# Routed feed-forward weights as four 32-column tiles with the shared matrix added on GpSimd, routing steps moved to the start, the bias split in attention, inputs ahead of constants

## The chip, the cores and the metric

One core of one Trainium2 chip runs the kernel as one program. The metric is the device time of one execution in microseconds (us), lower is better. The engines are named PE (TensorE, with its weight loads as PEld), DVE (the vector engine), ACT (ScalarE), POOL (GpSimd) and SP (SyncE, which issues the DMAs).

## The reference, cut to what matters

The input is 64 sequences of 375 frames with 16 features. Each is cut into 45 overlapping patches and projected to 64 features; then come four residual blocks, each behind a layer norm: attention (8 heads of 8), a dense top-2 mixture of 8 experts, a delta-rule recurrence, and the routed feed-forward block that the change is about:

```python
h = jax.nn.relu(flat @ Wi.T + bi)
for l in range(n_layers):                      # 2 layers
    shared = (jnp.einsum('nd,shd->snh', h, Ws[l]) + bs[l][:, None, :]).mean(axis=0)
    routed = jnp.zeros_like(h)
    for e in range(n_experts):                 # 16 experts, one per sequence
        ye = h @ Wr[l, e].T + br[l, e]
        routed = routed + jnp.where((route == e)[:, None], ye, 0.0)
    h = jax.nn.relu(shared + routed + h)
out = h @ Wo.T + bo
```

The expert is chosen per sequence by `route_id`, so all 45 tokens of a sequence use one 128x128 matrix `Wr[l, e]`; `Ws[l]` is shared by all; the residual `h` is an identity matrix more.

## The kernel before, in words

All activations stay in SBUF in one tensor `arena`, features on partitions, two sequences side by side (partitions 0 to 63 and 64 to 127). The 64 sequences are 32 such pairs in 4 chunks (`C`) of 8 pairs (`PP`); a chunk has `W` = 360 columns (8 pairs x 45 tokens `T`). `a(c, off, n)` is a piece of chunk `c`, `slot(i)` its i-th piece of 360 columns; `bank(c, b)` is one of its two PSUM banks. `K` holds the constants, in five groups that five DMAs load; `k(name)` is one of them.

The order of the work is one list, `ORDER` (lines 82 to 138), of steps (name, index, chunk). Every engine walks the same list and issues its own part of each step, so each engine's queue is in that order, and semaphores tie them together. Most stages run chunk 0, 1, 2, 3 of one step, then of the next. Attention (lines 99 to 112) runs 32 units (pair i, chunk c): step `t` transposes the probabilities, `s` makes the next scores (PE), their maximum and difference (DVE, lines 591 and 593), `e` the exponential (ACT, line 377), and `pv`, two units later, the weighted values. The recurrence (`m`, `lx`, `lt`, `u`, `y2`, `z`, `w`, `o`) works on 45x45 blocks per sequence. Each fp32 matrix product appears in the profile as two passes, each a weight load and a matmul. All products but the transposes (line 827) have line 763.

What the change touches:

- SP (lines 230 to 263): constants group 0, input chunk 0, group 1, the mask constants, input chunks 1 to 3, the route ids twice (`rid` on one row, `ridb` on 51), then groups 2, 3, 4. When DVE has made the expert indices `ride` (semaphore `r_id`), SP loads one 128x128 matrix for each of the 64 sequences and both layers (line 258): layer 0 into `WG0`, layer 1 into the arena behind `WG1_`, the latter once that chunk's attention is done (`h1`).
- POOL: after clearing buffers (lines 272 to 274) it adds the identity to both shared matrices (line 280); then come sums of the rotary products (285, 288), the 32 key products of attention (291) and later steps.
- DVE: `route_ids()` (lines 508 to 535) is called after the last value step of attention (line 587). Seven instructions (512 to 523) make `ride` and the one-hot matrix `oneh`; four more (527 to 534) split the biases into three bf16 parts, `rb_split`.
- PE, step `r` (lines 1005 to 1021), once per layer `i` and chunk `c`. For each of two banks j: one bf16 product adds the bias over all 360 columns, eight fp32 products of a sequence's 128x128 matrix with its 45 columns follow, and one fp32 product of the shared matrix (identity added) with all 360 columns ends the sum. ACT rectifies both banks (line 495).
- PE waits in step `f` for `r_oh`, `rb_split` and `wsI`, and in `r` for the weight DMAs.

## Time and profile before

| what | value |
|---|---|
| median of 3 runs | 418.08 us |
| lowest | 417.31 us |
| profiled execution, first to last instruction | 417.9 us |
| PE busy | 359.1 us (86%), 4976 passes |
| DVE busy | 226.4 us (54%) |
| ACT busy | 198.2 us (47%) |
| POOL busy | 112.6 us (27%) |
| DMA | 14.82 MB, mean 35 GB/s |

One of the three runs took 674.59 us, so only the median and the lowest are used. What the profiled execution took beyond its span is not listed; the median is 0.2 us above the span. Busy time of an engine says how long it had instructions in flight; the share is of the span. A timeline row gives start, length, engine, line, operation, tensors (out<-in), partitions x elements and a count, and in brackets the idle time before it and who ended it. The shape of a PE row reads rows*columns of the weights, then rows x columns of the moving operand.

### The profile page before, as it was taken

How to read it: one execution, taken by the hardware profiler on the slowest of the kernel's cores; microseconds unless marked ns; L12 is line 12 of the kernel's file. 1: busy time of each engine (PE TensorE's matmuls, PEld its weight loads, DVE VectorE, ACT ScalarE, POOL GpSimd, SP SyncE). 2: the span in 40 equal slices, each digit the busy share in tenths (PEclk: the TensorE clock that was granted, in tenths of full speed). 3: DMA queues.
4: the chain of work that ended last, by engine and by line, in shares of the span. 5: the costliest groups of instructions: out<-in, count | busy, mean ns of one | idle time of the engine just before them, and what ended most of it. 6: DMA issues, size and time to landing. Idle time of an engine off the chain costs nothing.

```text
span 417.9 us, 11928 instructions
## 1 busy us (share of the span) xinstructions
PE 359.1 (86%) x4976; PEld 247.0 (59%) x4976; DVE 226.4 (54%) x446; ACT 198.2 (47%) x382; POOL 112.6 (27%) x138
## 2 busy tenths in 40 slices
PE   4999839999997799999587947878776997999997
PEld 1447726677775534343244527878776993477774
DVE  3277797787646743333693999946663038500002
ACT  1574235444447356776747792570008645531110
POOL 9009991000000036465133026880000003000000
PEclk9999969999998699999959995999999898899999
DMA  7400012222212122121000000000000000000001
GB/s 280 192 0 2 5 38 57 60 59 59 65 54 61 55 62 59 58 64 57 20 0 0 2 0 2 3 4 5 5 5 3 3 5 0 2 0 2 0 2 71
DMA packets 20558, 14.82 MB, mean 35 GB/s; under 512 B 2329, under 2 KB 19353, under 8 KB 20377
## 3 DMA queue, kind: packets, MB, share of 16 engines
q1 hardware_dynamic: 20504, 14.07, 10.7%
q8 instruction: 39, 0.64, 0.7%
q14 instruction: 15, 0.11, 0.1%
HBM read 13.32 MB, written 0.74 MB: 34 GB/s over the span
## 4 chain that ended last, share of the span: by engine, by line
PE 54%; DVE 18%; POOL 11%; issue 8%; ACT 7%; DMA 1%; SPq 0%; POOLq 0%; DVEq 0%
PE PS L763 49%; POOL arena L298 7%; PE PS L827 4%; DVE arena L710 3%; DVE arena L566 2%; DVE arena L549 2%; POOL arena L321 2%; DMA arena<-xT 1%; ACT arena L356 1%; ACT arena L353 1%; POOL arena L317 1%; ACT arena L468 1%; POOL arena L316 1%; DVE arena L713 1%; ACT arena L472 1%
## 5 line engine op out<-in xcount | busy, mean ns | idle before, releaser
L763 PE MATMUL PS<-arena,K 128*128 128x360 f32 (+2 forms) x608 | 163.1, 513 | 21.5 <-DVE arena L566 6.4
L763 PE MATMUL PS<-arena 128*45 128x45 f32 (+6 forms) x3264 | 129.9, 227 | 21.3 <-ACT arena L448 9.7
L763 PEld LDWEIGHTS PS<-arena 128*45 128x45 f32 (+3 forms) x3264 | 111.7, 133 | 40.1 <-issue 23.9
L763 PEld LDWEIGHTS PS<-arena,K 128*128 128x128 f32 (+2 forms) x608 | 75.8, 183 | 82.5 <-issue 22.1
L298 POOL TENSOR_TENSOR arena<-arena 128x360 f32<-128x360 f32 x32 | 30.0, 948 | 105.9 <-DVE arena L672 105.2
L672 DVE TENSOR_TENSOR arena<-PS,arena 128x360 f32<-128x360 f32 x32 | 17.1, 533 | 33.7 <-ACT arena L402 33.7
L763 PE MATMUL PS<-K,arena 128*45 128x32 f32 (+4 forms) x768 | 26.1, 223 | 5.1 <-DVE arena L655 4.4
L763 PEld LDWEIGHTS PS<-K,arena 128*45 128x45 f32 (+2 forms) x768 | 25.3, 132 | 7.0 <-DVE arena L655 5.0
L827 PE MATMUL PS<-K,arena 128*128 128x128 f32 x128 | 21.5, 292 | 7.8 <-ACT arena L377 7.7
L756 DVE SCALAR_TENSOR_TENSOR arena<-PS,K,arena 128x360 f32<-128x360 f32 x4 | 2.4, 593 | 47.2 <-PE PS L763 47.2
L380 ACT COPY arena<-PS 128x360 f32<-128x360 f32 x32 | 14.9, 468 | 25.5 <-PE PS L827 25.4
L398 ACT ACTIVATE arena<-PS,K 128x720 f32<-128x720 f32 x32 | 24.9, 862 | 2.5 <-PE PS L763 2.5
L291 POOL TENSOR_TENSOR arena<-arena,K 128x360 f32<-128x360 f32 x32 | 24.6, 813 | 0.0
L495 ACT ACTIVATE arena<-PS 128x720 f32<-128x720 f32 x8 | 6.2, 771 | 38.6 <-PE PS L763 38.6
L324 POOL TENSOR_TENSOR arena<-arena 128x360 f32<-128x360 f32 x4 | 4.4, 1110 | 70.6 <-DVE arena L557 70.6
L543 DVE TENSOR_TENSOR arena<-arena,PS 128x360 f32<-128x360 f32 x24 | 12.3, 528 | 19.3 <-PE PS L763 18.3
L402 ACT COPY arena<-PS 128x360 f32<-128x360 f32 x32 | 14.8, 463 | 14.8 <-PE PS L763 14.8
L591 DVE TENSOR_REDUCE smax<-PS 128x8 f32<-128x360 f32 x32 | 17.0, 531 | 8.7 <-PE PS L763 8.6
L377 ACT ACTIVATE arena<-arena 128x360 f32<-128x360 f32 x32 | 16.4, 512 | 10.9 <-DVE arena L593 10.9
L549 DVE TENSOR_TENSOR arena<-arena 128x360 f32<-128x360 f32 x24 | 12.7, 531 | 14.8 <-ACT arena L356 14.8
L468 ACT ACTIVATE arena<-arena,K 128x360 f32<-128x360 f32 x8 | 4.3, 589 | 34.4 <-DVE arena L745 34.4
L827 PEld LDWEIGHTS PS<-K,arena 128*128 128x128 f32 x128 | 14.2, 145 | 10.2 <-ACT arena L377 8.2
(124 smaller groups left out, 422.8 us busy)
## 6 DMA issues: line engine op xcount, KB each, us to landing
WG<-wr SPq DMA_DIRECT2D x64, 64.0 KB, 1.9
arena<-wr SPq DMA_DIRECT2D x64, 64.0 KB, 1.9
arena<-xT SPq DMA_DIRECT2D x4, 368.0 KB, 6.4
K<-consts SPq DMA_DIRECT2D x1, 1171.0 KB, 12.3
K<-consts SPq DMA_DIRECT2D x1, 852.0 KB, 9.9
out<-arena SPq DMA_DIRECT2D x4, 180.0 KB, 1.9
K<-consts SPq DMA_DIRECT2D x1, 510.0 KB, 5.5
K<-consts SPq DMA_DIRECT2D x1, 352.0 KB, 12.4
```

The costliest lines, as they stand in the source:

```text
L291: g.tensor_tensor(a(c, KX_ + i * W).rearrange("q (h t) -> q h t", t=T), a(c, slot(4) + i * T, T).unsqueeze(1).broadcast_to([128, NH, T]), ...
L298: g.tensor_tensor(a(c, H_), a(c, H_), a(c, slot(3 + i % 2)), ALU.add).then_inc(sem["acc"], 1)
L377: s.activation(pb, pb, ACT.Exp).then_inc(sem["s_exp"], 1)
L380: s.copy(a(c, PT_, 512).rearrange("q (r t) -> q r t", t=64)[:, :, 0:T], bank(c, 1, 512).rearrange("q (r t) -> q r t", t=64)[:, :, 0:T]).th ...
L398: s.activation(halves(a(c, slot(6), 2 * W)), both(c), ACT.Gelu, bias=k("b1", i, i + 1)).then_inc(sem["gelu"], 1)
L402: s.copy(a(c, slot(8)), bank(c, 1)).then_inc(sem["cwb"], 1)
L549: v.tensor_tensor(a(c, dst), a(c, xc), a(c, sq), ALU.mult).then_inc(sem["ln_out"], 1)
L591: v.tensor_reduce(smax[:, c, :], sc, AX.X, ALU.max).then_inc(sem["s_max"], 1)
L672: v.tensor_tensor(a(c, slot(3 + i % 2)), bank(c, 0), a(c, slot(8)), ALU.mult).then_inc(sem["y_mul"], 1)
L710: v.scalar_tensor_tensor(out=kr[:, :, 0, 1:T], in0=pair(a(c, slot(3)))[:, :, 1:T], scalar=vec(f"feat{j}"), in1=pair(a(c, slot(13)))[:, :, ...
L763: return nc.tensor.matmul(o, l, r, start=start, stop=stop)
L827: last = nc.tensor.transpose(bank(c, 1, 128, 128 * g), a(c, PB_ + 128 * g, 128), k("identf"))
```

## The change

1. The eight fp32 products of a bank are each cut into four, with 32 columns of the weights and 32 output partitions each. Their sum no longer gets the product with the shared matrix, and both bias products come ahead of all of them.
2. POOL adds the shared matrix (with the identity) to all 16 loaded matrices of a chunk and layer in one instruction of 128x2048 elements, eight in all: those of layer 0 after the last key product of attention, those of layer 1 at the recurrence's first `lx` step. PE's `r` waits for that (`wsum`) in place of the DMAs.
3. The identity sums on POOL move from the start to behind the last key product.
4. `route_ids()` comes first on DVE, before the first layer norm, and loses the four split instructions; these (`split_biases()`) come after the 17th unit's values in attention.
5. SP issues all four input chunks and the route ids ahead of constants group 1 and the masks, and group 4 ahead of 2 and 3.

```diff
             load_consts(0)
             for c in range(C):
                 sp.dma_start(a(c, XT_, 2 * PP * CH), xT[:, c, :]).then_inc(sem[f"x{c}"], 16)
-                if c == 0:
-                    load_consts(1)
-                    sp.dma_start(KB[:], masks_bf).then_inc(sem["cst_bf"], 16)
...
+            load_consts(1)
+            sp.dma_start(KB[:], masks_bf).then_inc(sem["cst_bf"], 16)
+            for g in (4, 2, 3):
...
+            def shared_plus_identity():
...
+                for l in range(NL):
+                    ws = k("Ws", 128 * l, 128 * l + 128)
+                    g.tensor_tensor(ws, ws, k("identf"), ALU.add).then_inc(sem["wsI"], 1)
+            def add_shared(l, c):
+
+                pool.wait_ge(sem["wsI"], l + 1)
+                pool.wait_ge(sem[f"wg{l}_{c}"], 16 * 2 * PP)
+                w = WG0[:, 2 * PP * c:2 * PP * (c + 1), :] if l == 0 else a(c, WG1_, 2 * PP * 128).rearrange(
+                    "q (b n) -> q b n", n=128)
+                shared = k("Ws", 128 * l, 128 * l + 128).unsqueeze(1).broadcast_to([128, 2 * PP, 128])
+                g.tensor_tensor(w, w, shared, ALU.add).then_inc(sem["wsum"], 1)
...
+                    if (i, c) == (PP - 1, C - 1):
+                        shared_plus_identity()
+                        for cc in range(C):
+                            add_shared(0, cc)
...
+                elif name == "lx" and i == 0:
+                    add_shared(1, c)
...
+            route_ids()
...
-                    if c == C - 1:
-                        route_ids()
...
+                    if (i, c) == (PP // 2, 0):
+                        split_biases()
...
-                        pe.wait_ge(sem["wsI"], NL)
...
-                    pe.wait_ge(sem[f"wg{i}_{c}"], 16 * 2 * PP)
+                    pe.wait_ge(sem["wsum"], n)
                     src = slot(2 if i == 0 else 4)
                     for j in range(2):
                         mm(pair(bank(c, j)), rb_split[:, 1, 128 * i:128 * i + 128],
...
+                    for j in range(2):
                         for p in range(PP):
                             b = PP * j + p
-                            w = WG0[:, 2 * PP * c + b, :] if i == 0 else a(c, WG1_ + 128 * b, 128)
-                            mm(bank(c, j, T, p * T), w, a(c, src + j * W + p * T, T), start=False, stop=False)
-                        last = mm(bank(c, j), k("Ws", 128 * i, 128 * i + 128), a(c, src + j * W), start=False)
+                            for lo in range(0, 128, 32):
+                                w = WG0[:, 2 * PP * c + b, lo:lo + 32] if i == 0 else a(c, WG1_ + 128 * b + lo, 32)
+                                last = mm(bank(c, j, T, p * T, lo, lo + 32), w, a(c, src + j * W + p * T, T), start=False,
+                                          stop=(p == PP - 1))
```

How the instructions stand, first on PE for the routed step of one chunk in layer 0, before (`oneh` is the one-hot matrix, `WG0` the loaded matrices; a row counts products, each of which is one or two passes):

```order
L763 MATMUL PS<-arena,K 128x360 x28
L763 MATMUL PS<-oneh,rb_split 128x360
L763 MATMUL PS<-arena,WG0 128x45 x8
L763 MATMUL PS<-arena,K 128x360
L763 MATMUL PS<-oneh,rb_split 128x360
L763 MATMUL PS<-arena,WG0 128x45 x8
L763 MATMUL PS<-arena,K 128x360
```

and now, two chunks:

```order
L785 MATMUL PS<-arena,K 128x360 x28
L785 MATMUL PS<-oneh,rb_split 128x360 x2
L785 MATMUL PS<-arena,WG0 32x45 x64
L785 MATMUL PS<-oneh,rb_split 128x360 x2
L785 MATMUL PS<-arena,WG0 32x45 x64
```

The 16 products with 128 output rows and the two shared ones of a chunk have become 64 products with 32 output rows.

On DVE, the end of the value steps and the start of attention's units, before (`ride` is what SP waits for):

```order
L516 TENSOR_SCALAR oneh<-ridb,K 51x64
L519 TENSOR_TENSOR arena<-arena 1x64
L521 TENSOR_TENSOR arena<-arena 1x64
L523 TENSOR_SCALAR ride<-arena 1x64
L527 CAST rb_split<-K 51x256
L529 SCALAR_TENSOR_TENSOR K<-rb_split,K 51x256
L532 CAST rb_split<-K 51x256
L534 SCALAR_TENSOR_TENSOR rb_split<-rb_split,K 51x256
L591 TENSOR_REDUCE smax<-PS 128x8
```

and now the first instructions of DVE, with the split in the middle of attention:

```order
L523 TENSOR_SCALAR oneka<-K 128x1
L529 TENSOR_SCALAR arena<-rid 1x64
...
L540 TENSOR_SCALAR ride<-arena 1x64
L565 TENSOR_TENSOR arena<-arena,PS 128x360 x4
...
L623 TENSOR_TENSOR arena<-PS,orec 128x64
L548 CAST rb_split<-K 51x256
L550 SCALAR_TENSOR_TENSOR K<-rb_split,K 51x256
L553 CAST rb_split<-K 51x256
L555 SCALAR_TENSOR_TENSOR rb_split<-rb_split,K 51x256
L611 TENSOR_REDUCE smax<-PS 128x8
```

All eleven stood ahead of attention's first maximum; none does now.

On POOL, the rotary sums, the key products and what follows them, before:

```order
L280 TENSOR_TENSOR K<-K 128x128 x2
L285 TENSOR_TENSOR arena<-arena 128x360 x4
L288 TENSOR_TENSOR arena<-arena 128x360 x4
L291 TENSOR_TENSOR arena<-arena,K 128x360 x32
L298 TENSOR_TENSOR arena<-arena 128x360 x32
```

and now:

```order
L296 TENSOR_TENSOR arena<-arena 128x360 x4
L299 TENSOR_TENSOR arena<-arena 128x360 x4
L302 TENSOR_TENSOR arena<-arena,K 128x360 x32
L281 TENSOR_TENSOR K<-K 128x128 x2
L290 TENSOR_TENSOR WG0<-WG0,K 128x2048 x4
L313 TENSOR_TENSOR arena<-arena 128x360 x32
```

The four sums into the loaded matrices stand between the key products and the mixture's accumulations.

## Rows read from the trace of the kernel before

**Rows 1.** The page's first line.

```profile
span 417.9 us, 11928 instructions
```

**Rows 2.** Who TensorE waited for: us in total, times, longest us.

```profile
PE PS L763 <- issue: 6.6, 10, 0.8
...
PE PS L763 <- DVE PS L503: 5.3, 1, 5.3
```

**Rows 3.** Timeline, routed stage, layer 0, chunk 0: start us, us, instructions.

```profile
366.71 0.32 PE L763 MATMUL PS<-oneh,rb_split 51*128 51x360 bf16 x1
...
366.96 1.98 PE L763 MATMUL PS<-arena,WG 128*128 128x45 f32 x16
...
368.76 0.85 PE L763 MATMUL PS<-arena,K 128*128 128x360 f32 x2
...
369.55 0.33 PE L763 MATMUL PS<-oneh,rb_split 51*128 51x360 bf16 x1
```

**Rows 4.** The same view, ScalarE: the last rectification of the routed stage.

```profile
412.37 0.77 ACT L495 ACTIVATE arena<-PS 128x720 f32<-128x720 f32 x1 [4.92 <-PE PS L763]
```

**Rows 5.** Timeline, vector engine and TensorE, before attention's first transposes.

```profile
48.82 0.79 DVE L512 TENSOR_SCALAR arena<-rid 1x64 f32<-1x64 int32 x1
...
54.06 0.28 DVE L527 CAST rb_split<-K 51x256 bf16<-51x256 f32 x1
...
56.10 0.89 DVE L534 SCALAR_TENSOR_TENSOR rb_split<-rb_split,K 51x256 bf16<-51x256 bf16 x1
...
56.91 0.52 DVE L591 TENSOR_REDUCE smax<-PS 128x8 f32<-128x360 f32 x1
...
58.60 1.11 PE L827 MATMUL PS<-K,arena 128*128 128x128 f32 x4 [7.67 <-ACT arena L377]
```

**Rows 6.** The same view: the last of the first four score products.

```profile
50.16 0.77 PE L763 MATMUL PS<-arena 128*128 128x360 f32 x2
```

**Rows 7.** Engines' busy time by stretch; PEclk is the granted clock.

```profile
60.00:61.00 1.00, 1.00 (x3) 0.37 (x2) 0.97 (x3) 0.51 (x1) 1.00 (x2) 0.50 0.21 63
...
61.00:62.00 1.00, 1.00 (x7) 0.98 (x6) 0.73 (x3) 0.92 (x3) 1.00 (x2) 0.78 0.21 61
```

**Rows 8.** Timeline, attention in its steady part, two successive maxima.

```profile
72.81 0.53 DVE L591 TENSOR_REDUCE smax<-PS 128x8 f32<-128x360 f32 x1 [0.32 <-PE PS L763]
...
74.61 0.53 DVE L591 TENSOR_REDUCE smax<-PS 128x8 f32<-128x360 f32 x1 [0.32 <-PE PS L763]
```

**Rows 9.** Timeline of the first 16 us: products of the four input chunks.

```profile
5.25 2.68 PE L763 MATMUL PS<-arena,K 128*64 128x360 f32 x8 [5.25 <-DVE PS L503]
...
8.90 11.28 PE L763 MATMUL PS<-arena,K 128*64 128x360 f32 x40 [0.97 <-DMA arena<-xT]
...
13.95 0.56 ACT L344 ACTIVATE arena<-PS,K 128x360 f32<-128x360 f32 x1 [1.75 <-PE PS L763]
...
15.18 0.56 ACT L344 ACTIVATE arena<-PS,K 128x360 f32<-128x360 f32 x1 [0.67 <-PE PS L763]
```

**Rows 10.** Timeline of TensorE, recurrence: two unbroken runs of 128 passes.

```profile
289.97 2.92 PE L763 MATMUL PS<-arena 128*45 128x45 f32 x128 [0.81 <-issue]
...
293.43 2.92 PE L763 MATMUL PS<-arena 128*45 128x45 f32 x128 [0.54 <-issue]
```

**Rows 11.** DMA queues from 286 to 319 us: packets, MB, share.

```profile
q8 instruction: 9, 0.15, 2.0%
```

**Rows 12.** Timeline of TensorE, recurrence output, 64-column weights.

```profile
336.80 7.06 PE L763 MATMUL PS<-arena 128*64 128x45 f32 x235
```

**Rows 13.** Timeline of TensorE, the values of attention.

```profile
37.72 10.06 PE L763 MATMUL PS<-K,arena 128*45 128x32 f32 x256
```

**Rows 14.** Line 258: count, duration ns min/median/max, first and last start.

```profile
L258 SPq DMA_DIRECT2D WG<-wr x64: 332/333/1192, 55.1 to 127.6; - x64
```

**Rows 15.** GpSimd: key products in the timeline; then groups by line.

```profile
39.78 24.62 POOL L291 TENSOR_TENSOR arena<-arena,K 128x360 f32<-128x360 f32 x32
...
L324 POOL TENSOR_TENSOR arena<-arena 128x360 f32<-128x360 f32 x4 | 4.4, 1110 | 70.6 <-DVE arena L557 70.6
```

More of the change, by code:

```diff
@@ L64 @@
 SEMS = """rb_steps r_steps g_steps cst0 cst1 cst2 cst3 cst4 cst_bf ids psum0 init oneka rb_split
-r_id r_oh wsI
+r_id r_oh wsI wsum
 tok_mm tok_y h0 ln_mean ln_xc ln_sq ln_var ln_log ln_rs ln_out
@@ L238, in _ @@
                 sp.dma_start(a(c, XT_, 2 * PP * CH), xT[:, c, :]).then_inc(sem[f"x{c}"], 16)
-                if c == 0:
-                    load_consts(1)
-                    sp.dma_start(KB[:], masks_bf).then_inc(sem["cst_bf"], 16)
             sp.dma_start(rid[:], route[0:1, :]).then_inc(sem["ids"], 16)
             sp.dma_start(ridb[:], route[0:1, :].broadcast_to([3 * (NR + 1), B])).then_inc(sem["ids"], 16)
-            for g in (2, 3, 4):
+            load_consts(1)
+            sp.dma_start(KB[:], masks_bf).then_inc(sem["cst_bf"], 16)
+            for g in (4, 2, 3):
                 load_consts(g)
@@ L274, in _ @@
                 g.memset(a(c, VD_, PP * 2 * NKV * 18), 0.0).then_inc(sem["init"], 1)
-            pool.wait_ge(sem["cst4"], 16)
-            pool.wait_ge(sem["cst1"], 16)
-            for l in range(NL):
-                ws = k("Ws", 128 * l, 128 * l + 128)
-                g.tensor_tensor(ws, ws, k("identf"), ALU.add).then_inc(sem["wsI"], 1)
+            def shared_plus_identity():
+                pool.wait_ge(sem["cst4"], 16)
+                pool.wait_ge(sem["cst1"], 16)
+                for l in range(NL):
[8 more added lines that the diff above has]
+                g.tensor_tensor(w, w, shared, ALU.add).then_inc(sem["wsum"], 1)
             for name, i, c in ORDER:
@@ L523, in route_ids, with split_biases @@
                 v.tensor_scalar(ride[:], rtmp[:, 0, :], float(NR), None, ALU.add).then_inc(sem["r_id"], 1)
+            def split_biases():
+                rows = 3 * (NR + 1)
                 dve.wait_ge(sem["cst4"], 16)
```

## The prediction

> **What bounds the kernel now.** I began with the length of the span, 417.9 us [rows 1], then asked who TensorE waits for. It is in flight 86% of the time, and the named waits are small; the interesting ones are 6.6 us on "issue", in ten pieces, and 5.3 us at the start for the clearing of PSUM [rows 2]. So TensorE's own stream is the bound in most stages, and I read three places of the timeline.
>
> First the routed stage. It starts with a bias product at 366.71 [rows 3] and its last rectification starts at 412.37 [rows 4]: 45.7 us for eight steps (4 chunks, 2 layers), 5.7 us each, with nothing between them. Inside one bank, the sixteen passes over 128-column weights take 368.76 - 366.96 = 1.80 us, so 112 ns each, although each moves only 45 columns. The shared matrix and the turn to the next bias take 369.55 - 368.76 = 0.79 us, a bias 0.25 us [rows 3]. The stage pays for loading weights, not for streaming.
>
> Second the start of attention. From 48.82 to 56.91 the vector engine makes route ids and splits biases; only then comes the first maximum, and TensorE starts the first transposes at 58.60 after 7.67 us of idleness [rows 5]. The scores that the maximum reads were long there: the last of the first four ended at 50.16 + 0.77 = 50.93 [rows 6]. After the pause the granted clock is 0.50 (the 1.2 GHz level) and returns within the stretch 61 to 62, whose mean is 0.78 [rows 7].
>
> Third the first 16 us: TensorE begins at 5.25, when PSUM is clear, and then waits 0.97 us for input chunk 1 [rows 9].
>
> **The routed stage, part by part.** Removed per step: 32 passes over 128 columns and 4 over the shared matrix. Added: 128 passes with 32-column weights and the same 45 moving columns. Nothing in this trace has 32-column weights cycling over four column tiles. The nearest rows are the recurrence's: 45-column weights, 45 moving columns, outputs alternating between the two halves of the partitions. There 128 passes take 2.92 us, 22.8 ns each [rows 10]. With 64-column weights, also alternating, 7.06 us for 235 is 30.0 ns [rows 12]. Without alternation, the values of attention, 45-column weights and 32 moving columns: 10.06 us for 256, 39.3 ns [rows 13]. Alternating tiles thus nearly halves the price, so loads into one tile do proceed beside work in the other. I take 22.8 ns, since 32 columns are nearest to 45 and the tiles alternate still more; the bounds are 22.8 below (a cheaper pass stands nowhere in these rows) and 39.3 above.
>
> A step is then 128 x 22.8 ns = 2.92 us, two biases at 0.25 us, and one turn from the small passes back to a bias, at most about 0.5 us (the 0.79 us less 0.3 us for streaming two passes of 360 columns at 2.4 GHz): 3.4 to 3.9 us.
>
> There is a second limit. In rows 10 each run is exactly 128 passes, that is 256 instructions, and is followed by 0.54 to 0.81 us in which TensorE waits for nothing that the profile shows. In the 33 us from 286 to 319 the instruction queue moved 9 packets of 0.15 MB together [rows 11], some 16 KB each; one per 33 / 9 = 3.67 us. I read this as instruction fetch: 128 passes cannot go by in less than about 3.67 us. A step has 130 passes, 3.73 us, as much as its work. I take 3.8 us: 8 x 3.8 = 30.4 us instead of 45.7, a gain of 15.3 us. Bounds: 8 x 3.4 = 27.2 (gain 18.5) and, at 39.3 ns with 1.0 us beside, 8 x 6.03 = 48.2 (a loss of 2.5).
>
> The Trainium skill, page "TensorE: Matmul & The Clock Gate", section on LDWEIGHTS, gives a load as its columns divided by 1.2 per ns. By it 32 columns cost 26.7 ns and four of them as much as one load of 128, so that cutting into tiles saves no load at all; the stage would be an estimated 8 x (3.42 + 1.0) = 35.4 us and the whole 5.0 us later than mine. Rows 12 speak against taking it as a floor for alternating tiles: 64 columns are 53.3 ns by the rule and took 30.0.
>
> **The shared sums on POOL.** A sum over 2048 columns is not in the trace. Key products took 24.62 / 32 = 0.77 us for 360 columns, the dearest sum 1110 ns [rows 15]: per column 2.1 to 3.1 ns, so 4.4 to 6.3 us each, eight of them 35 to 50 us. They are off the path if their inputs come early and POOL has room. Layer 0: POOL is free after its key products, at 39.78 + 24.62 = 64.4; SP needs (127.6 - 55.1) / 63 = 1.15 us per matrix [rows 14], 18.4 us a chunk, and starting near 15 us is done with the fourth chunk near 89. The POOL sums end by about 95, long before POOL's next work in the mixture. Layer 1 sits behind POOL's last work for the recurrence's setup and needs 18 to 25 us from about 280, while `r` wants it from 367 on. Cost on the path: nothing. If POOL were twice as slow there would still be room.
>
> **Route ids and bias split.** With them gone, the first maximum can start at 48.82, its chain to the transposes is 58.60 - 56.91 = 1.69 us long, which gives 50.51; TensorE is busy until 50.93. So the transposes begin there, 7.7 us earlier. And there is no pause, so the half clock from 58.6 to about 61.4 (0.78 is 0.44 us at half and the rest at full) goes too: 2.8 us of work at half speed is 1.4 us. What is late next is TensorE itself.
>
> The seven id instructions move behind the arrival of the ids. They took 54.06 - 48.82 = 5.24 us while POOL was running [rows 5]. The ids now stand behind 1.6 MB instead of 2.4 MB, so I put them near 9 to 10 us; done by 12 to 15. The vector engine is first wanted by the layer norm after the fourth input chunk, near 13 to 14. I count 0, at worst 1.5 us. The four split instructions take 56.91 - 54.06 = 2.85 us in attention. A unit there is 74.61 - 72.81 = 1.80 us, with 0.32 us of idleness of the vector engine [rows 8], and its differences are wanted by transposes four units later. A delay of 2.9 us fits into that distance of 7 us and is caught up at 0.32 us a unit: 0, at worst 2.9.
>
> **Inputs first.** The 0.97 us wait goes. Chunk 3 took 15.18 - 13.95 = 1.23 us, while chunk 0 took 2.68 [rows 9]; the faster passes may also start earlier when TensorE has no break. Between 0.5 and 2.7 us, I take 1.5. Constants group 1 is now behind the inputs but first wanted near 28.
>
> **Sum.** 15.3 + 7.7 + 1.4 + 1.5 = 25.9 us. From the span of 417.9 us that is 392.0; the median stands 0.2 above the span, which I leave within the rounding: 392.
>
> **Rivals.**
> (a) Fetch does not bind and the turns are free, 3.4 us a step: 418 - 10.6 - 18.5 = 389. For it: the first buffer is full when the stage starts. Against: nine fetches in a row at one spacing.
> (b) Four tiles overlap no better than rows 12, 30.0 ns: 8 x (3.84 + 1.0) = 38.7, gain 7.0, time 400. At the 39.3 ns of rows 13: 410, within the noise of nothing gained but attention's part.
> (c) The other side: POOL holds the vector engine for the length of an instruction. For it: tiny instructions on one row took 0.79 us while POOL's key products took 0.77 [rows 5, 15]. Were all vector work held, four sums of 4.4 us or more in attention and four in the recurrence would cost 2 x 17.6 = 35 us there: 427 or more. It decides from the point where over 26 us are held. Against: the maximum took 0.52 us beside a running POOL and 0.53 beside an idle one [rows 5, 8]; what reads PSUM is not held, and in both places nearly all vector work reads PSUM.
> (d) A pass costs what an instruction costs, whatever its columns. At the 112 ns of rows 3 the stage is 8 x (14.3 + 1.0) = 122 us and the time about 418 - 10.6 + 77 = 484; the break-even is (45.7 + 10.6) / 8 - 1.0 over 128, 47 ns. Against: 22.8 ns was reached. The Trainium skill, page "TensorE: Matmul & The Clock Gate", section "Back-to-back issue gap", names some 62 ns per matmul where the sequencer decodes each in software; by that the time would be an estimated 433 us. The trace disagrees by its 22.8 ns.
> (e) The change does not do what it says at the start: ids arrive so late that the first layer norm waits some 4 us: 396.
>
> **How the numbers follow.** Forecast 0.54, (a) 0.17, (b) 0.19 at 400 and 0.03 at 410, (c) 0.03, (d) 0.02, (e) 0.02. A measurement of this kernel can tell about 2% from no change, which is 8.4 us, so faster means below 409.7: 0.54 + 0.17 + 0.19 + 0.02 + 0.01 = 0.93; same 0.04; slower 0.03. The range goes from 386 (case (a) with the full 2.7 us of the start) to 401 (case (b)).
>
> **What would show it.** Right: a routed step of about 3.8 us with gaps of half a microsecond after every 128 passes; TensorE without a pause before the transposes and a granted clock of 1.00 there; SP's weight loads from about 15 us; POOL sums of 4 to 6 us ending before 100 and 310. Wrong: a routed pass above 30 ns, vector instructions in attention longer than 0.55 us while POOL sums run, a wait of `r` for a sum, or a first layer norm later than 15.5 us.

## The result and the profile after

The changed kernel takes 392.52 us, the median of four runs (390.86 to 395.19), against 418.95 us for the kernel before. The ratio is 0.936, 95% interval 0.932 to 0.941: 6.4% faster. The forecast was 392.0 us. The number was right to 0.5 us, but one term of it was not: the price of a pass in the routed stage was put at twice what it is, and instruction fetch, which the prediction also had, held the stage's total. Medians here count every execution, the ratios leave out one slow one each of the kernel before (674.59 us), of two tiles (526.71) and of the old transfers (401.88).

First the page of the changed kernel: its length, the busy times and the granted clock in 40 slices. TensorE is busy 326.8 us instead of 359.1, although it runs 736 more passes; GpSimd is busy 142.3 us instead of 112.6.

```profile
span 393.2 us, 13416 instructions
...
PE 326.8 (83%) x5712; PEld 222.4 (57%) x5712; DVE 220.6 (56%) x446; ACT 197.7 (50%) x382; POOL 142.3 (36%) x146
...
PEclk9999999999997799999959998699999999879996
```

The last digit of the clock row is 6, and was 9 before: the grant is lower at the very end. That is followed up below.

The routed stage in the timeline, the third step of layer 0 and the start of the next. Rows 3 answer to these; lines 785 and 512 are lines 763 and 495 of the kernel before.

```profile
361.89 0.37 PE L785 MATMUL PS<-arena,WG 128*32 128x45 f32 x15 [1.50 <-issue]
...
362.19 0.48 PE L785 MATMUL PS<-oneh,rb_split 51*128 51x360 bf16 x2
...
362.60 1.35 PE L785 MATMUL PS<-arena,WG 128*32 128x45 f32 x111
...
365.99 0.39 PE L785 MATMUL PS<-arena,WG 128*32 128x45 f32 x17 [2.04 <-issue]
...
366.32 0.48 PE L785 MATMUL PS<-oneh,rb_split 51*128 51x360 bf16 x2
```

111 passes run in 1.35 us, then TensorE does nothing for 2.04 us in which it "waits for nothing that the profile shows", then come 17 more, and the step is over. So passes cost 11 to 12 ns, and about half of this step (2.04 of 4.13 us) is a pause in the middle of it. In the successive steps 113, 111, 108, 106, 103, 101 and 98 passes stand ahead of the pause: since a step has 130 passes, the pause comes after every 128, and wanders through the steps. The seven pauses are 1.44 to 2.04 us long, 1.7 us in the mean, and between 357 and 386 us the queue that brings instructions moved seven packets:

```profile
q8 instruction: 7, 0.11, 1.4%
```

The first step has no pause:

```profile
357.15 1.51 PE L785 MATMUL PS<-arena,WG 128*32 128x45 f32 x128
...
358.60 0.48 PE L785 MATMUL PS<-oneh,rb_split 51*128 51x360 bf16 x2
```

It takes 358.60 - 356.75 = 1.85 us. The whole stage, from its first bias at 356.75 to its last rectification, is 385.98 - 356.75 = 29.2 us against 45.7 before.

```profile
385.87 4.39 PE L785 MATMUL PS<-arena,K 128*64 128x360 f32 x16
...
385.98 0.77 ACT L512 ACTIVATE arena<-PS 128x720 f32<-128x720 f32 x1 [3.64 <-PE PS L785]
```

Behind it the last sixteen passes of the kernel take 4.39 us; before they were over in less than 3.4. The tail from the last rectification to the end is 393.2 - 386.0 = 7.2 us; before it was 417.9 - 412.4 = 5.5 [rows 4]. The busy times by stretch say why: the granted clock is 1.00 for most of the stage and 0.62 in its last 4.5 us, where it falls to the 1.2 GHz level, and it is 0.50 until 388 us.

```profile
362.20:381.50 19.30, 10.55 (x657) 8.08 (x652) 0.00 (x0) 3.85 (x5) 0.00 (x0) 1.00 0.01 4
...
381.50:386.00 4.50, 2.85 (x133) 2.27 (x134) 0.00 (x0) 0.79 (x2) 0.00 (x0) 0.62 0.01 4
```

Where this fall comes varies. The changed routed step ran in three more profiles (values alternate, and the old transfers twice). There the clock, over stretches of 2 us, was at 0.50 to 0.59 from 364 to 368, from 368 to 374 and from 378 to 382 us, in the middle of the stage; the stage took 28.6, 29.2 and 27.3 us, and the tail 5.5 us each time. So the 1.7 us of the tail belong to this one execution. In all four TensorE had been idle for much of the time at a grant of 1.00 before the fall (here 8.75 of the 19.3 us from 362.2). The kernels here whose routed stage has no pauses show no such fall in it, save one, the sum alone at full width.

The start of attention, to be held against rows 5 and 6: the first maximum follows the value steps at once, and the transposes (line 849, before 827) begin as soon as TensorE is through the first four scores.

```profile
46.64 0.51 DVE L611 TENSOR_REDUCE smax<-PS 128x8 f32<-128x360 f32 x1
...
47.98 0.77 PE L785 MATMUL PS<-arena 128*128 128x360 f32 x2
...
48.59 0.60 PE L849 MATMUL PS<-K,arena 128*128 128x128 f32 x4
...
52.73 0.65 PE L849 MATMUL PS<-K,arena 128*128 128x128 f32 x4
```

58.60 has become 48.59, 10.0 us earlier. The fourth group of transposes, which stood at 64.16 in the kernel before, starts at 52.73, 11.4 us earlier: the 1.4 us of half clock are gone as well. Of the 10.0 us, 2.2 were there already at the first layer norm, which starts at 13.81 instead of 15.98; 7.8 are the pause.

```profile
5.25 12.76 PE L785 MATMUL PS<-arena,K 128*64 128x360 f32 x48 [5.25 <-DVE PS L520]
...
10.83 0.18 DVE L529 TENSOR_SCALAR arena<-rid 1x64 f32<-1x64 int32 x1 [5.57 <-DMA ridb<-route]
...
11.85 0.18 DVE L540 TENSOR_SCALAR ride<-arena 1x64 int32<-1x64 f32 x1
...
13.01 0.56 ACT L361 ACTIVATE arena<-PS,K 128x360 f32<-128x360 f32 x1 [0.68 <-PE PS L785]
...
13.81 2.34 DVE L565 TENSOR_TENSOR arena<-arena,PS 128x360 f32<-128x360 f32 x4 [1.78 <-PE PS L785]
```

TensorE no longer waits for input chunk 1 [rows 9]. The ids land at 10.8 us, and the seven id instructions take 12.0 - 10.8 = 1.2 us where they took 5.24 [rows 5]; they are done at 12.03, before the vector engine is wanted at 13.81.

The bias split in attention and the one wait it caused, in the timeline of the vector engine and of TensorE:

```profile
82.55 0.28 DVE L548 CAST rb_split<-K 51x256 bf16<-51x256 f32 x1
...
83.69 0.47 DVE L555 SCALAR_TENSOR_TENSOR rb_split<-rb_split,K 51x256 bf16<-51x256 bf16 x1
...
84.09 0.52 DVE L611 TENSOR_REDUCE smax<-PS 128x8 f32<-128x360 f32 x1
...
85.70 0.63 PE L849 MATMUL PS<-K,arena 128*128 128x128 f32 x4 [0.53 <-DVE arena L623]
```

1.5 us of split instead of 2.85, and TensorE waits 0.53 us once for the values' normalisation (line 623).

The sums on GpSimd, in the groups by line:

```profile
L290 POOL TENSOR_TENSOR WG<-WG,K 128x2048 f32<-128x2048 f32 x4 | 15.2, 3816 | 13.2 <-DMA WG<-wr 13.2
...
L290 POOL TENSOR_TENSOR arena<-arena,K 128x2048 f32<-128x2048 f32 x4 | 15.2, 3842 | 0.0
```

3.8 us each, under the 4.4 to 6.3 estimated. The last of layer 0 ends at 90.7, the last of layer 1 at 284.9, 72 us before the routed stage begins. The one real wait among them, 13.2 us, is GpSimd's own for the fourth chunk's matrices, and costs nobody anything.

### The profile page after: what moved, and what is told of

It is laid out like the page before. It is cut to its first block, busy times and chain, and to the rows that moved or that the text cites. A ratio compares the mean times of both kernels' runs of the same rounds, so it can differ in the third digit from the quotient of the medians.

```text
span 393.2 us, 13416 instructions
## 1 busy us (share of the span) xinstructions
PE 326.8 (83%) x5712; PEld 222.4 (57%) x5712; DVE 220.6 (56%) x446; ACT 197.7 (50%) x382; POOL 142.3 (36%) x146
## 4 chain that ended last, share of the span: by engine, by line
PE 52%; DVE 17%; issue 12%; ACT 10%; POOL 8%; POOLq 0%; DVEq 0%
PE PS L785 48%; POOL arena L313 7%; PE PS L849 4%; DVE arena L588 2%; DVE arena L732 2%; DVE arena L571 2%; ACT arena L373 2%; ACT arena L370 1%; ACT arena L476 1%; ACT arena L485 1%; DVE PS L520 1%; ACT arena L489 1%; ACT arena L365 1%; DVE arena L735 1%; DVE arena L584 1%
## 5 line engine op out<-in xcount | busy, mean ns | idle before, releaser
L785 PE MATMUL PS<-arena,K 128*128 128x360 f32 (+2 forms) x576 | 149.7, 515 | 21.2 <-DVE arena L588 7.3
L785 PE MATMUL PS<-arena 128*45 128x45 f32 (+6 forms) x3648 | 118.5, 221 | 31.7 <-issue 15.4
L785 PEld LDWEIGHTS PS<-arena 128*45 128x45 f32 (+4 forms) x3648 | 100.7, 127 | 50.6 <-issue 36.4
L785 PEld LDWEIGHTS PS<-arena,K 128*128 128x128 f32 (+2 forms) x576 | 71.0, 183 | 81.8 <-issue 22.6
L365 ACT ACTIVATE arena<-arena 128x360 f32<-128x360 f32 x24 | 11.8, 503 | 17.1 <-DVE arena L565 15.7
L290 POOL TENSOR_TENSOR WG<-WG,K 128x2048 f32<-128x2048 f32 x4 | 15.2, 3816 | 13.2 <-DMA WG<-wr 13.2
L394 ACT ACTIVATE arena<-arena 128x360 f32<-128x360 f32 x32 | 16.4, 513 | 3.3 <-DVE arena L613 3.3
## 6 DMA issues: line engine op xcount, KB each, us to landing
K<-consts SPq DMA_DIRECT2D x1, 1171.0 KB, 10.7
```

The costliest lines, as they stand in the source:

```text
L290: g.tensor_tensor(w, w, shared, ALU.add).then_inc(sem["wsum"], 1)
L365: s.activation(a(c, sq), a(c, xc), ACT.Square).then_inc(sem["ln_sq"], 1)
L394: s.activation(pb, pb, ACT.Exp).then_inc(sem["s_exp"], 1)
L785: return nc.tensor.matmul(o, l, r, start=start, stop=stop)
```

## Experiments

Most expectations name a theory A and a rival B. The stage means the time from the first bias of the routed steps to the start of their last rectification. The medians stand in one table; the kernel before took 420.05 and 419.18 us beside the first and the second four.

| kernel | median us | ratio to before (95%) | stage us | pass |
|---|---|---|---|---|
| changed | 392.52 | 0.936 (0.932 to 0.941) | 29.2 | 11 ns and pauses |
| two tiles of 64 | 384.08 | 0.913 (0.905 to 0.920) | 19.4 | 31 ns |
| tile by tile | 404.5 | 0.963 (0.956 to 0.969) | 38.8 | 35 ns |
| sum, full width | 423.51 | 1.008 (1.004 to 1.012) | 57.3 | 116, then 218 ns |
| moves only | 409.35 | 0.973 (0.966 to 0.981) | 45.7 | 112 ns |
| combined | 377.23 | 0.902 (0.894 to 0.910) | 19.4 | 31 ns |
| values alternate | 387.28 | 0.922 (0.915 to 0.928) | 28.6 | 11 ns and pauses |
| old transfers | 394.73 | 0.937 (0.928 to 0.945) | 29.2 | 11 ns and pauses |
| two tiles, shared product | 398.69 | 0.951 (0.944 to 0.957) | 34.1 | 33 ns |

**Two tiles of 64 columns.**

```diff
-                            for lo in range(0, 128, 32):
+                            for lo in range(0, 128, 64):
```

(the slices of weights and of output partitions follow, 64 wide)

> The changed kernel with two 64-column tiles in place of four of 32. Theory A (instruction fetch bounds the routed stage, one fetch of 128 passes per 3.7 to 4.1 us): a step has 66 passes, so fetch allows 1.9 to 2.1 us; the passes cost the 30.0 ns of the recurrence's 64-column weights, 64 x 30 = 1.9 us, with 0.6 to 0.85 us beside them 2.5 to 2.8 us. The stage falls from 29.2 us to about 21, the clock stays at 1.00 to the end (1.7 us more), whole kernel 383 to 385 us. Rival B (the pauses are something of each step, such as turning from narrow weights back to the full-width bias): a step keeps its 1.5 to 2.0 us pause, 1.9 + 0.85 + 1.8 = 4.6 us, stage 36 us, kernel about 400 us.

```profile
359.80 0.48 PE L785 MATMUL PS<-oneh,rb_split 51*128 51x360 bf16 x2
...
360.21 2.07 PE L785 MATMUL PS<-arena,WG 128*64 128x45 f32 x64
...
362.21 0.48 PE L785 MATMUL PS<-oneh,rb_split 51*128 51x360 bf16 x2
```

A step takes 362.21 - 359.80 = 2.41 us, with no pause in it, and is the same in all eight. The passes are nearly three times as dear as those over 32 columns (2.0 us for 64, 31 ns), yet the kernel is 8.4 us faster than the changed one. Half as many instructions go by, and the pauses go with them. That fits instruction fetch and not a pause that belongs to a step, which would have made the stage 36 us. The granted clock is 1.00 over the whole stage. Theory A had 21 us, 19.4 were measured; its 383 to 385 us held.

**Tile by tile.**

```diff
-                        for p in range(PP):
-                            b = PP * j + p
-                            for lo in range(0, 128, 32):
+                        for lo in range(0, 128, 32):
+                            for p in range(PP):
+                                b = PP * j + p
```

> The changed kernel with the same 64 products of 32 columns per step, but all eight sequences of one column tile before the next tile. Theory A (the 11 ns of a pass come from work in different tiles going on at once): consecutive passes in one tile cost 27 to 39 ns, a step 3.5 to 5.0 us plus 0.85 us, stage 35 to 47 us, kernel 398 to 410 us, and the pauses inside a step shrink or go, since the passes then take longer than their fetch. Rival B (narrow weights are cheap by themselves): passes stay at 11 ns and the time at 393 us within 1%.

```profile
363.94 4.49 PE L785 MATMUL PS<-arena,WG 128*32 128x45 f32 x128
...
368.37 0.48 PE L785 MATMUL PS<-oneh,rb_split 51*128 51x360 bf16 x2
```

Exactly the same products in another order: a pass costs 4.43 / 128 = 35 ns instead of 11, as theory A had it, and the pauses are gone: 128 passes now last 4.43 us, longer than the 3.6 to 4.1 us from one block to the next in the changed kernel. The queue again moved seven packets in the stage. So narrow weights are not cheap by themselves. The price falls when the next product goes to another column tile, and it falls threefold over four tiles. The number of passes is that of the changed kernel, so this is also the plainest sign that the pauses belong to the rate of instructions and not to their kind. The granted clock is 1.00 over the whole stage.

**The sum alone, full width.**

```diff
-                            for lo in range(0, 128, 32):
-                                w = WG0[:, 2 * PP * c + b, lo:lo + 32] if i == 0 else a(c, WG1_ + 128 * b + lo, 32)
-                                last = mm(bank(c, j, T, p * T, lo, lo + 32), w, a(c, src + j * W + p * T, T), start=False,
-                                          stop=(p == PP - 1))
+                            w = WG0[:, 2 * PP * c + b, :] if i == 0 else a(c, WG1_ + 128 * b, 128)
+                            last = mm(bank(c, j, T, p * T), w, a(c, src + j * W + p * T, T), start=False,
+                                      stop=(p == PP - 1))
```

> The changed kernel with full 128-column weights, the shared matrix still added on GpSimd: parts the removed shared product from the tiles. Theory A: a step is 32 passes of 112 ns, 3.6 us, two biases 0.5 us and a turn of 0.2 to 0.5 us, 4.3 to 4.6 us; stage 34.5 to 37 us against 45.7 before and 29.2 changed; kernel 396 to 399 us. Of the stage's 16.4 us the sum is then worth 9 to 11 and the tiles 5 to 7. Rival B (the shared product cost only its streaming, 0.3 us a bank): stage 41 us, kernel 403 us.

Both theories missed, to the same side: 423.5 us against 396 to 399 and 403. The timeline and the clock by stretch:

```profile
357.06 3.77 PE L785 MATMUL PS<-arena,WG 128*128 128x45 f32 x32
...
368.36 7.05 PE L785 MATMUL PS<-arena,WG 128*128 128x45 f32 x32
...
357.00:360.00 3.00, 3.00 (x28) 2.94 (x27) 0.00 (x0) 1.33 (x2) 0.00 (x0) 1.00 0.00 0
...
362.00:370.00 8.00, 8.00 (x37) 7.33 (x37) 0.00 (x0) 0.77 (x1) 0.00 (x0) 0.50 0.00 0
...
370.00:400.00 30.00, 30.00 (x134) 27.33 (x134) 0.00 (x0) 3.08 (x4) 0.00 (x0) 0.50 0.00 1
```

The first step runs as theory A had it: 32 passes in 3.7 us, 116 ns each with the turn behind them. In the second step, just before 362 us, the granted clock falls to 0.50, the 1.2 GHz level, and stays there to the end of the stage and into the tail; from the third step on a pass costs 6.98 / 32 = 218 ns. TensorE had no idle time in this stretch at all. Before the fall it did nothing but load 128 columns of weights and move 45 through them, with two bias products a step. The next experiment has the same 32 passes and two biases, and the four passes of the shared product over 360 columns besides, and keeps 1.00 from end to end. In the routed stage the two kernels differ by that product and by the order of the biases (both ahead, or one ahead of each bank); with the product gone the stage is 57.3 - 45.7 = 11.6 us slower. Both biases ahead and no shared product are found in the two kernels above too, which keep 1.00, so neither brings the clock down by itself; with 128-column loads they come together with the fall. Which of the two does it there was not parted. That the shared product kept the clock up is the likelier reading, and not shown.

**The moves only.** The routed step of before, no sums on GpSimd, the other parts of the change kept.

```diff
-                        for cc in range(C):
-                            add_shared(0, cc)
...
-                elif name == "lx" and i == 0:
-                    add_shared(1, c)
...
-                    pe.wait_ge(sem["wsum"], n)
+                    pe.wait_ge(sem[f"wg{i}_{c}"], 16 * 2 * PP)
...
+                            mm(bank(c, j, T, p * T), w, a(c, src + j * W + p * T, T), start=False, stop=False)
+                        last = mm(bank(c, j), k("Ws", 128 * i, 128 * i + 128), a(c, src + j * W), start=False)
```

> The changed kernel with the routed step of before (full width, shared product, no sums on GpSimd): only the moves of route ids, bias split and transfers are left. Theory A: the moves are worth 10.0 us at the start of the routed stage and nothing after it; time 407 to 409 us, with the stage at 45.7 us and the tail at 5.5 us. Rival B (the long sums on GpSimd hold up attention or the recurrence in the changed kernel by some us): the routed stage then starts more than 1 us earlier than the 356.8 us of the changed kernel, and the time is 406 us or less.

```profile
356.10:400.80 44.70, 44.70 (x304) 34.38 (x301) 0.00 (x0) 7.08 (x10) 0.00 (x0) 1.00 0.00 1
...
85.89 0.63 PE L845 MATMUL PS<-K,arena 128*128 128x128 f32 x4 [0.54 <-DVE arena L619]
```

409.35 us: the moves are worth 2.7% of 420.05 (1.9 to 3.4%), 10.7 us, and the routed stage and its clock are as before. The wait of 0.54 us in attention is there without any sum on GpSimd, so the split causes it; in the combined kernel below, which has the split elsewhere, TensorE has no wait there. Theory B is not borne out: the time is 409 us and not 406 or less, and the stage starts at 356.1 against 356.75 with the sums. Such starts differ by 5 us between the profiles that leave the values alone (353.9 to 358.9), so a hold-up of a microsecond or two would not be seen.

**Combined.** Three edits on the changed kernel: the two tiles above, the loop order of the next experiment, and the split at the recurrence's step `u`.

```diff
-                    if (i, c) == (PP // 2, 0):
-                        split_biases()
...
+                elif name == "u" and c == 0:
+                    split_biases()
```

> The changed kernel with three edits at once: two 64-column tiles in the routed stage, the values of attention with the two output halves alternating, and the bias split in the recurrence, where the vector engine idles over 10 us. From the two-tile kernel's 384.1 us: 2.7 to 4.2 us less for the values and 0.5 us for the split, 379 to 381 us. If the value edit brings nothing, 383.5 us.

377.23 us, the best of the study, 9.8% below the kernel before; 1.8 us better than the lower end expected. The single gains, 8.4 us for the two tiles, 5.2 for the values and 0.5 for the split, make 14.1; measured are 15.3 below the changed kernel. The 0.5 us for the split is the wait seen in the trace and was not measured alone.

**The values of attention, alternating.**

```diff
-                    for hh in range(2):
-                        for p, j in pairs:
+                    for p, j in pairs:
+                        for hh in range(2):
```

> The changed kernel with only the loop order of attention's 256 value passes changed, so that each next product goes to the other half of the output partitions. Theory A (work in different column tiles overlaps, and fetch allows one pass per 28.6 ns at best over 128 of them): the 256 passes fall from 10.06 us to 5.8 to 7.3 us, kernel 388.5 to 390 us. Rival B (the passes wait for the vector engine's and ScalarE's evictions of the values anyway): attention's first transposes start less than 1 us earlier, kernel within 1 us of 392.5.

```profile
34.96 5.74 PE L785 MATMUL PS<-K,arena 128*45 128x32 f32 x256
...
40.71 0.32 PE L785 MATMUL PS<-KB 128*128 128x360 bf16 x1
```

To be held against rows 13: the same 256 passes take 5.74 us instead of 10.06, 22.4 ns each, which is the pace of rows 10. The kernel gains 5.2 us on the changed one (387.28), more than the 2.5 to 4 expected. The passes account for 4.3 of it, with a duration just under theory A's 5.8 us; the rest is within what executions differ by. The first maximum starts at 42.3 instead of 46.6 us. No pause showed in this profile. 256 passes are only two blocks, and the wide passes before them are slow, so instructions may have been fetched ahead; that is argued and not tested. In the combined kernel's profile there is one of 0.53 us in the same place.

**Old transfer order.**

```diff
+                if c == 0:
+                    load_consts(1)
+                    sp.dma_start(KB[:], masks_bf).then_inc(sem["cst_bf"], 16)
...
-            load_consts(1)
-            sp.dma_start(KB[:], masks_bf).then_inc(sem["cst_bf"], 16)
-            for g in (4, 2, 3):
+            for g in (2, 3, 4):
```

> The changed kernel with the transfer order of before. Theory A (inputs first are worth the 0.97 us wait and the earlier full clock, 2.2 us together): chunk 3's product leaves at 15.2 us instead of 13.0, the first layer norm at 16.0 instead of 13.8, kernel 394.5 to 395.5 us. Rival B (the ids then come late, since 2.4 MB stand ahead of them, and hold the first layer norm): the layer norm's first subtraction starts after 16.5 us, kernel 396 us or more.

```profile
8.44 7.78 PE L786 MATMUL PS<-arena,K 128*64 128x360 f32 x34 [0.51 <-DMA arena<-xT]
...
10.79 0.18 DVE L530 TENSOR_SCALAR arena<-rid 1x64 f32<-1x64 int32 x1 [5.53 <-DMA ridb<-route]
...
13.84 2.34 DVE L566 TENSOR_TENSOR arena<-arena,PS 128x360 f32<-128x360 f32 x4 [1.85 <-PE PS L786]
```

Neither theory: TensorE waits 0.51 us for input chunk 1, and the first layer norm starts at 13.84, as with the new order. The ids are not late either. The time is 394.73 against 392.52 us, and the intervals of the two ratios overlap nearly whole (0.928 to 0.945, 0.932 to 0.941). So the 2.2 us at the start are hardly the transfers' doing. Two more profiles, of the kernel before itself and of this one, were taken to see how much the start varies.

> The kernel before once more, for its profile. Its first layer norm started at 15.98 us, that of the kernel with the old transfer order but ids first at 13.84. Theory A (when TensorE's passes get twice as fast at the start varies from execution to execution, whatever the transfer order): the first layer norm starts somewhere from 13.5 to 16 us, not again at 15.98 within 0.1. Rival B (the ids-first order or the transfers set it): 15.98 again.

> The changed kernel with the transfer order of before, once more, for its profile. Theory A (variation from execution to execution): TensorE waits 0.5 to 1.0 us for input chunk 1 as in both profiles with that order, and the first layer norm starts between 13.5 and 16 us. Rival B: 13.84 again.

The two took 417.03 and 393.64 us, one execution each. Rows of the kernel before:

```profile
8.15 8.04 PE L763 MATMUL PS<-arena,K 128*64 128x360 f32 x33 [0.22 <-DMA arena<-xT]
...
14.10 2.35 DVE L543 TENSOR_TENSOR arena<-arena,PS 128x360 f32<-128x360 f32 x4 [8.85 <-PE PS L763]
```

The unchanged kernel itself starts its first layer norm at 14.10 in this execution (its span 415.3 us), with a wait of 0.22 us for chunk 1; the changed kernel with the old order gave 0.22 us, less than the 0.5 expected, and 13.57. Over the ten profiles of changed kernels in this study, eight with the new order and two with the old, it was 12.65 to 14.04. The rest is when the passes of the first products become twice as fast, which differed from execution to execution. The old transfer order costs its wait, 0.2 to 1.0 us, and of the 2.2 us between the two first profiles the larger part was chance.

**Two tiles with the shared product.** The moves-only kernel with 64-column tiles and no sums on GpSimd.

```diff
-                            w = WG0[:, 2 * PP * c + b, :] if i == 0 else a(c, WG1_ + 128 * b, 128)
-                            mm(bank(c, j, T, p * T), w, a(c, src + j * W + p * T, T), start=False, stop=False)
+                            for lo in range(0, 128, 64):
+                                w = WG0[:, 2 * PP * c + b, lo:lo + 64] if i == 0 else a(c, WG1_ + 128 * b + lo, 64)
+                                mm(bank(c, j, T, p * T, lo, lo + 64), w, a(c, src + j * W + p * T, T), start=False,
+                                   stop=False)
```

> Two 64-column tiles in the routed stage, but with the shared product on TensorE and no sums on GpSimd, the moves as in the changed kernel. Theory A: a bank is a bias of 0.25 us, 32 passes of 31 ns and 0.79 us for the shared product and the turn, 2.0 us, a step 4.1 us against 2.41 us with the sum; stage 33 us, clock at 1.00, kernel 395 to 398 us. So the sum is worth 13 us once the passes are cheap. Rival B (the narrow passes need the sum's one long run, and two turns a step cost more): a step is 5 us or more, kernel 403 us or more.

```profile
357.54 1.14 PE L781 MATMUL PS<-arena,WG 128*64 128x45 f32 x32
...
358.60 0.87 PE L781 MATMUL PS<-arena,K 128*128 128x360 f32 x2
...
359.41 0.33 PE L781 MATMUL PS<-oneh,rb_split 51*128 51x360 bf16 x1
```

A bank is 359.41 - 357.29 = 2.12 us, a step 4.24, the stage 34.1 us, the kernel 398.69, all just above theory A's figures. The shared product and its turn cost 0.81 us a bank beside cheap passes and 0.79 beside dear ones [rows 3]. With two tiles the sum on GpSimd is worth 398.69 - 384.08 = 14.6 us; alone, at full width, it costs 14.2 (423.51 against 409.35). The two parts of the routed edit are not a sum of two gains: the sum pays only with tiles.

## Why the prediction came out

**The routed stage: the limit right, the work in it wrong.** Its total was put at 30.4 us and is 29.2. The mis-sized term is the price of a pass: "I take 22.8 ns" from the recurrence's rows, with 22.8 called the lower bound. It is 11 ns (1.39 us of weight loads for 128). The recurrence alternates over two tiles, this stage over four, and taking turns among four tiles halves the price again (its weights are also narrower, 32 columns against 45; tile by tile they cost 35). So the step's own work is 1.85 us, not 3.4 to 3.9. What held the total was the second limit: one fetch per 3.67 us from rows 10 and 11. The measured distances between the blocks of 128, from 361.89 to 385.12, are six in 23.23 us, 3.87 us each, and 130 passes therefore 3.93. Seven such steps are 0.9 us more than the forecast's seven of 3.8, and the first step, which went by without a pause, is 1.95 us less than its 3.8; these two small errors partly cancel. The forecast had the fetch at "as much as its work"; it is twice the work. Since fetch was the longer of the two, the wrong price changed nothing in the total; had it not bound, the forecast would have been far off. Rival (a), in which fetch does not bind, is out, and its 389 us rested on the same wrong price: without pauses the stage would be 8 x 1.85 = 15 us.

**The rule on weight loads.** The row says 11 ns for a pass over 32 columns when tiles alternate, and 35 when they don't. The Trainium skill, page "TensorE: Matmul & The Clock Gate", section "LDWEIGHTS (loading the stationary operand)", has the rule of columns over 1.2, 26.7 ns for 32 columns. The 35 ns stand above it and the 11 ns far below, so the rule is no floor for tiles that take turns. That cutting saves no load was the prediction's conclusion from it: it holds tile by tile, where four passes of 35 ns cost more than one of 112, and not when the tiles alternate. The same page's 62 ns per matmul, section "Back-to-back issue gap", is out as well, by the same 11 ns.

**Instruction fetch.** The rows say some 16 KB per 128 passes (seven packets, 0.11 MB) and one block every 3.55 to 4.10 us. The Trainium skill, page "Runtime: NRT & Kernel Launch", section "Instruction fetch mechanics", has the same block of 256 instructions and calls the cost of crossing one mostly hidden. It is hidden here at 35 ns a pass; at 11 the pauses take 11.9 of the 29.2 us.

**Attention.** "The transposes begin there, 7.7 us earlier" was 7.8; the 1.4 us of half clock were 1.4. The moves-only kernel has both.

**The bias split at nothing.** The failed step is "its differences are wanted by transposes four units later". So they are, but the normalised values, which stand in the same queue, are wanted only two units later. It cost 0.5 us. It ran in 1.5 us and not 2.85, at a time when GpSimd was idle; the same instructions were slow before in the company of the key products. Rival (c) was half right in that way: instructions with all operands in SBUF were slow beside GpSimd (the seven id instructions 5.24 us against 1.2), those that read PSUM were not; the maximum took 0.53 us during the sums. The combined kernel agrees: there the ids came at 7.96 us, while GpSimd still cleared buffers, the first three id instructions were in flight until 10.5 and all seven took 3.4 us.

**Inputs first at 1.5 us.** Not shown. The two profiles differ by 2.2 us there, but the kernel before, profiled again, was only 0.3 us behind. The transfers account for the wait for chunk 1, 0.2 to 1.0 us.

**What was left out.** The clock at the end of the stage: it fell there in this execution, and the tail cost 1.7 us more; in the three other profiles with this routed step it fell earlier and the tail cost nothing. And the recurrence: between its setup and its last level the lead shrank from 10.8 to 8.3 us, because its pauses were 0.54 to 1.08 us in this execution against 0.53 to 0.81 before (they vary so between the profiles of all kernels here), and it came back to 10.0 at the recurrence's end, because the granted clock over the last 19 us of the recurrence was 1.00 in this profile and 0.91 in that of before, 1.7 us of work. At the routed stage the lead was 9.96 us against 10.6 forecast. The sum by the traces is 9.96 + 16.4 - 1.7 = 24.7 us, the difference of the spans, where the forecast had 25.9.

**How much of the hit was luck.** The forecast took 25.9 us from a span and read the result as a median, since "the median stands 0.2 above the span". All times in these runs stand 1.7 to 2.1 us above the span of the same execution (395.19 against 393.2), so by an estimate the profiled execution of the kernel before took some 419.8 us. From there the sum gives 393.9, from the median of 418.08 it gives 392.2. Single executions of the changed kernel lie 4.3 us apart. An error of 0.5 us is thus less than the method can promise. The lower end of the range was also mis-added: case (a), 389, with 2.7 us at the start in place of 1.5 is 387.7 and not 386; the result lies inside either way.

## What to carry to other kernels

When many small products with large weights follow each other, let each go to another column tile than the last: the prices here fit a load that goes on beside the work in the other tiles, and the loop order alone was worth a factor of 1.75 (attention's values) to 3 (the routed passes). But count instructions too: in a long stream below some 30 ns per pass (3.9 us over 128) the instructions are the bound, so take the widest tiles that reach that pace, here two of 64 columns and not four of 32. And before a wide product is taken out of a stage of small ones, ask what it does for the granted clock.

## What the runs showed of the hardware that was not expected

- A pass over 32-column weights with 45 moving columns costs 11 ns when four tiles take turns, and 35 ns when one tile is used eight times in a row. Over 64-column weights in two tiles it costs 31 ns, over 128 columns 112 ns.
- At the 1.2 GHz level a pass over 128-column weights with 45 moving columns costs 218 ns against 116. Weight loads are in flight for over 90% of either stretch, so the load goes with the granted clock.
- TensorE fell to the 1.2 GHz level without a moment of idleness, in a stream of 128-column loads with 45 moving columns each. The two-tile kernel, without wide products too, keeps 1.00 over its 19.4 us. So does the kernel tile by tile over 38.8 us. What in the stream decides was not tried further.
- One block of 128 passes of instructions came every 3.45 to 4.1 us when nothing else held the stream.
- The first layer norm of the kernel before started at 15.98 us in one execution and at 14.10 in another; 0.75 us of that was the longer wait for chunk 1, the rest came with when the first passes became twice as fast.
